# Transposing the normalised rows by DMA instead of on the matrix engine, tiles two to eight, in an eight-core recurrent block

## What is computed

```
xn  = layernorm(x)
s   = rwkv6_block(xn)            # token shift, 5 mixes, r/k/v/g/decay projections,
                                 # chunked recurrence (chunk 32, 4 heads), group norm, out projection
h   = silu(xn @ (wg/127).T) * (xn @ (wu/127).T)      # 1024 -> 3072, integer weights
g   = silu(h @ (wd/127).T)                           # 3072 -> 1024
out = x + s * g
```

## Time and profile before

| | us |
|---|---|
| time, median of 2 runs | 1740.55 (1739.62 to 1741.47) |
| the profiled execution's own time | 1747.32 |
| its span on the slowest core (core 5) | 1745.7 |
| spans of the eight cores | 1723.7 to 1745.7 |
| mean granted clock, both dies | 0.995 and 0.994 |
| busy: PE / PEld / DVE / ACT / POOL | 1673.4 / 780.0 / 1086.7 / 480.4 / 195.3 |
| moved by DMA, in the span | 303.47 MB |

### The profile page before, as it was taken

The page is one execution under the profiler, slowest core; times in us unless marked ns, Lnnn a source line. Parts: engine busy times, 40 slices in busy tenths (PEclk is TensorE's granted clock), DMA queues, the critical chain, the costliest instruction groups (busy, mean ns, idle before and its releaser), DMA issues.

```text
span 1745.7 us, 26548 instructions; the slowest of 8 cores (1723.7 to 1745.7 us)
## 1 busy us (share of the span) xinstructions
PE 1673.4 (96%) x9248; PEld 780.0 (45%) x9248; DVE 1086.7 (62%) x1844; ACT 480.4 (28%) x806; POOL 195.3 (11%) x408
## 2 busy tenths in 40 slices
PE   5899899999999999899999999999999999999998
PEld 2344344445444454343544445444454445544454
DVE  5475755657656577464775657757476485764756
ACT  1143211333114321142211432114321143212421
POOL 3111401112011020010200001000110001100000
PEclk9999899999999999999999999999999999999999
DMA  9999999997699877997436884465634355354412
GB/s 164 168 160 178 205 238 161 147 206 204 145 168 179 218 221 169 191 192 254 170 98 169 205 285 149 129 187 151 259 121 162 128 182 204 118 182 138 176 62 110
DMA packets 79234, 303.47 MB, mean 174 GB/s; under 512 B 10687, under 2 KB 15232, under 8 KB 73728
## 3 DMA queue, kind: packets, MB, share of 16 engines
q0 software_dynamic: 27456, 95.08, 34.5%
q10 hardware_dynamic: 25344, 124.79, 20.6%
q1 hardware_dynamic: 26304, 81.90, 13.6%
HBM read 348.56 MB, written 44.04 MB: 225 GB/s over the span
## 4 chain that ended last, share of the span: by engine, by line
PE 80%; DMA 10%; DVE 4%; issue 2%; ACT 1%; DVEq 1%; POOL 1%; SPq 1%; ACTq 0%; POOLq 0%
PE PB L1240 16%; PE PB L1245 15%; PE PB L1365 8%; PE PB L1354 7%; PE PB L1527 6%; PE PB L1504 6%; PE PB L1397 6%; PE PB L1466 3%; PE PB L1450 3%; DMA sb_wd<-kept_wd 3%; DMA sb_gu<-w_gu 3%; DMA sb_gu<-kept_gu 2%; DMA sb_wd<-w_fd 1%; PE PB L1273 1%; DVE sb_xin L920 1%
## 5 line engine op out<-in xcount | busy, mean ns | idle before, releaser
L1240 PE MATMUL PB<-sb_xnT,sb_gu 128*128 128x512 bf16 x1536 | 369.6, 384 | 25.8 <-DMA sb_gu<-w_gu 11.1
L1245 PE MATMUL PB<-sb_xnT,sb_gu 128*128 128x512 bf16 x1536 | 365.9, 381 | 0.0
L920 DVE SCALAR_TENSOR_TENSOR sb_xin<-PB,sb_xb,sb_dT 128x512 bf16<-128x512 f32 x320 | 218.0, 744 | 171.1 <-PE PB L1273 170.6
L691 ACT ACTIVATE sb_scr<-PB 128x512 bf16<-128x512 f32 x192 | 113.8, 597 | 560.1 <-PE PB L1245 540.2
L1240 PEld LDWEIGHTS PB<-sb_xnT,sb_gu 128*128 128x128 bf16 x1536 | 141.6, 98 | 214.6 <-issue 68.4
L1245 PEld LDWEIGHTS PB<-sb_xnT,sb_gu 128*128 128x128 bf16 x1536 | 151.4, 99 | 184.6 <-issue 6.1
L852 DVE SCALAR_TENSOR_TENSOR sb_hall<-PB,sb_scr 128x512 bf16<-128x512 f32 x192 | 130.6, 684 | 142.9 <-ACT sb_scr L691 142.7
L1365 PE MATMUL PB<-sb_wd,sb_hall 128*128 128x512 bf16 x768 | 179.8, 383 | 8.5 <-DMA sb_wd<-kept_wd 4.9
L1354 PE MATMUL PB<-sb_wd,sb_hall 128*128 128x512 bf16 x768 | 179.6, 383 | 6.9 <-DMA sb_wd<-w_fd 5.7
L459 POOL DMA_DIRECT2D sb_gu<-w_gu x106 | 57.5, 543 | 623.2 <-PE PB L1245 557.2
L700 ACT ACTIVATE sb_wc<-PB 128x512 bf16<-128x512 f32 x64 | 38.2, 597 | 316.2 <-PE PB L1365 316.2
(11 more groups left out here) (155 smaller groups left out, 1683.5 us busy)
## 6 DMA issues: line engine op xcount, KB each, us to landing
sb_gu<-w_gu POOLq DMA_DIRECT2D x106, 512.0 KB, 10.9
sb_gu<-kept_gu ACTq DMA_DIRECT2D x86, 512.0 KB, 4.9
sb_wd<-kept_wd ACTq DMA_DIRECT2D x56, 768.0 KB, 7.7
sb_ring<-kept_ring ACTq DMA_DIRECT2D x34, 1024.0 KB, 7.3
sb_xin<-x SPq DMA_DIRECT2D x48, 512.0 KB, 8.5
kept_gu<-sb_gu SPq DMA_DIRECT2D x24, 512.0 KB, 9.2
sb_ring<-w_g POOLq DMA_DIRECT2D x20, 512.0 KB, 13.0
sb_ring<-w_v POOLq DMA_DIRECT2D x16, 512.0 KB, 14.2
```

Of the source, the lines that this page charges most:

```text
L691: e.activation(out=sb_scr[:, p, :], in_=GB[p][:], func=AF.Silu, bias=0.0, scale=INV127).then_inc(a_silu, 1)
L920: e.scalar_tensor_tensor(out=sb_xin[:, p, c, :], in0=PM[j][:], scalar=sb_xb[:, n, c:c + 1], in1=sb_dT[:, c, :], op0=ALU.add, op1=ALU.mult) ...
L1240: e.matmul(GB[p][:], sb_gu[:, sl, 0, c, :], sb_xnT[:, c, :], start=(c == 0), stop=(c == NC - 1))
L1245: i = e.matmul(UB[p][:], sb_gu[:, sl, 1, c, :], sb_xnT[:, c, :], start=(c == 0), stop=(c == NC - 1))
```

## The change

Tile one is transposed as before. For tiles two to eight the eight PE transposes and the DVE copy of each block are gone; SP issues eight DMA transposes per block instead, each of 128x128 bf16 elements (32 KB), straight from `xnt` to `sb_xnT`, so 4 x 8 = 32 per tile and 224 in all. The semaphores `d_xT[j % 2]` count them (128 per block). They are placed in SP's program behind `load_x(it+1, 2)` (block 0), behind `load_x(it+1, 3)` (blocks 1 and 2) and behind `load_res(it, 3)` (block 3). PE's and DVE's first reads of `sb_xnT` wait for all 32 landings, and `ln_xnt` waits for the landing of the transposes that last read its buffer.

```diff
+    d_xT = [S("d_xT0"), S("d_xT1")]
+        def transpose_xn(it, j):
+            e.wait_ge(v_xnt, 4 * it + j + 1)
+            if j == 0:
+                e.wait_ge(t_gu, NHC * it)
+            for c in range(NC):
+                e.dma_start(sb_xnT[:, c, j * 128:(j + 1) * 128],
+                            xnt[j % 2][:, c * 128:(c + 1) * 128],
+                            transpose=True).then_inc(d_xT[j % 2], 16)
...
             if nxt:
                 load_x(it + 1, 2)
+                transpose_xn(it + 1, 0)
             for g in range(4):
                 keep_wd(it, 0, g)
             if nxt:
                 load_x(it + 1, 3)
+                transpose_xn(it + 1, 1)
+                transpose_xn(it + 1, 2)
             keep_ring(it, 6)
             keep_ring(it, 7)
...
             load_res(it, 2)
             load_res(it, 3)
+            if nxt:
+                transpose_xn(it + 1, 3)
             store_out(it, 0)
...
         def ln_xnt(it, j):
-            if n >= 2:
+            if n >= 6:
+                e.wait_ge(d_xT[j % 2], 128 * ((n - 4) // 2))
+            elif n >= 2:
                 e.wait_ge(t_xn, n - 1)
...
-        def copy_xnT(it, j):
-            ...
         def shift_and_xin0(it):
...
+            else:
+                e.wait_ge(d_xT[0], 256 * it)
+                e.wait_ge(d_xT[1], 256 * it)
...
                 evac_o(it, t)
-                if nxt:
-                    copy_xnT(it + 1, t)
...
         def gate_up(it, hc):
             if hc < 2:
-                e.wait_ge(v_xnT, 4 * (it + 1))
-                if it:
+                if it == 0:
+                    e.wait_ge(v_xnT, 4)
+                else:
+                    e.wait_ge(d_xT[0], 256 * it)
+                    e.wait_ge(d_xT[1], 256 * it)
...
         def ks_transpose(it, t):
-            elif it + 1 < N_MT:
-                e.wait_ge(v_xnT, 4 * (it + 1) + t)
             else:
                 e.wait_ge(a_ksT, 4 * it + t)
...
                 out_and_kv(it, t)
-                if nxt:
-                    xn_transpose(it + 1, t)
```

More of the change, by code:

```diff
@@ L1212, in xn_transpose @@
                 e.wait_ge(d_id, 16)
-            if it:
-                e.wait_ge(a_ksT, 4 * (it - 1) + j + 1)
-            elif j >= 2:
+            if j >= 2:
                 e.wait_ge(v_xnT, n - 1)
-            dst = P_tr if it else P_first[j % 2]
+            dst = P_first[j % 2]
             for c in range(NC):
```

## The result

| | us | ratio to before, 95% interval |
|---|---|---|
| before | 1740.55 (2 runs) | |
| changed kernel | 1750.94 (1750.57 to 1751.31, 2 runs) | 1.0057 [1.0036, 1.0077] |
| changed kernel again, on another occasion | 1752.34, before 1737.94 | 1.0075 [1.0055, 1.0095] |

The change makes the kernel slower by 0.6 to 0.75%, 10 to 13 us. In some executions the cores of one die run at a lower granted clock and take longer; all times and ratios here are of executions without that, and of the one profile that had it (`t2_late`) I read the other die's cores.

A forecast was written before the change was run, and what follows sets the result against it. PE was taken to bound the kernel, except where it soon waits for a DMA. Net removal -10.8, tile one +2 and crowded weight loads +10 gave +1.2 us on 1740.55, about 1742 us; range 1724 to 1800.

The forecast's parts named there:

- the removal: PE transposes gone from tiles two to eight: gross 15.4 us saved, net 10.8 after waits for weights take some back.
- t3: Tail stretch of block 3 on PE: removing its eight transposes was to save 0.44 us per tile.
- PE busy down by about 18 us: Sign that the steps are right: PE's busy time on the profile page falls by about 18 us.
- Crowding of the down-weight loads: Block 2's transposes fall into down-weight loads PE waits for: 2 us per tile, five tiles, +10 us; bounds +4 and +24.
- e: Time one transpose holds the DMA engines: taken as 0.25 us, between 0.10 by bytes and 0.59 by packets.
- SP's pace and block 3: SP's queue: eight issues at 0.62 us plus 6.7 us landing, 11.7 us, so block 3's transposes stay hidden.
- with 9 us over: Block 3's slack: 20.7 us until the first gate matmul, against 11.7 us needed for its transposes.
- rival 3: SP cannot keep pace above 1.7 to 1.75 us per transpose, block 3 late; 1792 us at 2.0 us; chance 0.28.
- the first of the two readings: The skill's 1.3 us is only issue pace: block 3 needs 17.2 us, under 20.7, and the sum stands.
- Tile one: `keep_wd` copies queue behind block 0's transposes on SP, delaying POOL's casts: +2 us once, bounds 0 and +8.
- the new wait of `ln_xnt` is cheap: DVE's wait before block 2's rows, written at 1280.94: block 0's transposes land by 1266.4, so no delay.
- Rival 2: Transposes crowd the weight loads, e = 0.6 us: +24 us in five windows, 1749 to 1762 us; chance 0.17.

The follow-up runs named there:

- t2_late: Block 2's transposes issued behind the second pair of residual loads, just ahead of block 3's, against the changed kernel's order; measured 1.0140 of before, +24 us.

## Why the prediction came out as it did

**What bounds the kernel, and the removal: right.** PE first, with savings lost where a DMA is awaited soon after. -10.8 forecast, -7.3 measured (interval to -9.9), -10.2 in the spans; the one term off is t3. My sign "PE busy down by about 18 us" did not come: it is 13.1 us with the removal alone and 7.6 us in the first profile of the changed kernel, whose matmuls ran slower in the stretches at 0.81.

**Crowding of the down-weight loads: right in place and nearly in size, but not by the mechanism of the sum.** I forecast +10 us over five tails, as eight transposes times e = 0.25 us on the engines; e is 0.30. The t2 stretches of the six tails behind the first grew by 9.0 us in the first profile and 8.6 in the second, and by 0.1 with the removal alone. That looks like e, but the kernel with one DMA per block holds the engines as long and has about a third of the late delay. So the near agreement is partly luck: the delay goes with many small transposing DMAs on the loads (224 of them +8 us in the late t2, as many plain copies +1.6, 28 larger transposes +2.5), and by what means they delay the loads is open. That block 1's group overlaps the loads too I had not seen, because I let it take 5 us where it takes 10.6.

**SP's pace and block 3: the step that was mis-sized.** "They come about 13.7 us apart and take 5 us to issue" and "with 9 us over" took 0.62 us per issue and 6.7 us to landing from the plain copies of the earlier trace rows. A transpose takes 1.25 us to issue where nothing holds it up. In the late tails that is hidden, as I wrote. In the first three tails the groups of block 3 took 21.08, 19.50 and 17.46 us, 2.6, 2.4 and 2.2 us each, and PE waited 4.16, 2.77 and 1.41 us; in the other four, at 1.25 to 1.4 us, it did not wait. So rival 3's threshold (1.7 to 1.75 us) held, but its reason is only half right. In tails two and three the slow pace is itself a sign of the queue: block 3's transposes land right behind the residual load, which lands late because 2 MB of copies now leave 30 us later than before; with block 2 on PE and with one DMA per block, where they leave earlier, those two tails have no lateness. I had let those copies wait, as their readers come "a whole stage later", and had not put block 3 behind them in the same queue. What makes tail one's load slow (no such copies, but casts on the engines) no run takes apart, and none issues block 3's group ahead of the residual loads. So rival 3's outcome came in three tails of seven, by 6 to 8 us, and the forecast's in four. I had weighed it over all seven, with one number.

The earlier trace rows would not have told the tails apart by themselves: nine slices are full, to 393 us, and not ten; tails two and three lie in slices of 6 to 8 tenths, and the engines are about half busy only from some 830 us on.

The Trainium skill (VectorE: DVE Perf Modes, "The three transpose paths") gives 1309 ns for such a transpose. The trace agrees with it as a pace of issue in the late tails (1.25 to 1.35 us), and it is no time on the engines (0.30 us): the first of the two readings that I weighed. The Trainium skill (Advanced Engine Details and Errata, "X-Bar Transpose (TRN2)") says that transposing DMAs are as fast as regular ones; here the trace differs: 1.25 against 0.6 to 0.8 us to issue, and 0.30 against 0.17 us on the engines for 128 x 128.

**Tile one: too small.** +2 for `keep_wd` behind block 0. POOL's last casts did wait for the copies, but shortly (1.73 and 1.58 us), and with the copies first, 4 us of that tail's +6 stay from t3 on. I also wrote that the new wait of `ln_xnt` is cheap, from the late tail. There it is; in tile one DVE stood in it 10.88 us. PE waited for nothing of DVE's in that tail.

**Sum.** +1.2 forecast, +10 and +13 measured: 3.5 us of the difference is the smaller removal, and the remaining 6 to 8 us are block 3's lateness and tile one, in the first three tails. The sign of the forecast was a near-zero sum of three large terms, and its range rested on the rivals: that the time lies inside it says little. Rival 2 was also added up wrong: 1740.6 - 10.8 + 24 is 1754, so its band was 1754 to 1762, and the measured 1751 lies below it.

## To carry to other kernels

Price a kind of DMA that the trace lacks by its issue and its engine time apart, by stage, and together with what stands ahead of it and behind it in its queue: the same group was late only where slow copies or loads stood ahead of it. Fold small transposes into one DMA before judging the idea: 28 in place of 224 turned a loss into nothing, and together with keeping the fullest tail on PE into a gain of 0.5%. When an experiment's total says little, look at its stages: moving one group out of the queue let another collide with the same loads.

## What the hardware showed that I had not expected

- A DMA transpose of 128 x 1024 bf16 holds SP's queue for 1.24 to 1.59 us in the late tail, about as long as one of 128 x 128; eight of the latter take 10.0 us. In tile one the one took up to 13.1 us and the eight up to 23.
- For the same rows of 256 bytes, transposing made each small packet dearer: 30 ns in the mean against 19 ns for the plain copy, and 42 ns in the DMAs of 128 x 1024, which none the less held up the down-weight loads less than the small ones did.
- What SP issued landed in order: block 3's first transpose 0.1 to 0.5 us behind the residual load issued before it, whether that load took 5 us or 25 us.
- Four cores of one die showed three or four stretches of 15 us at a granted clock of 0.81 (between its two levels, 1.2 and 2.4 GHz; PE was busy throughout them) in one profile, and none of them in another profile of the same kernel, whose time was no better.
